# Gated attention block on one core: row sums in the addition, variance by Square, a second buffer of x in the memory of contexts 0 and 1, and the next x's statistics in the middle of a batch

## The reference, cut

```python
# x (4, 512, 512), ctx (4, 512, 256), Wq, Wk (128, 256), weight (512, 512)
def block(x, ctx, g_xattn, g_ffn, ...):
    q = ctx @ Wq.T + bq;  k = ctx @ Wk.T + bk
    attention = softmax(q @ k.T)                       # 512 x 512 per batch
    x = x + tanh(g_xattn) * (layernorm(x) @ attention.T)
    h = layernorm(x)                                    # no affine part
    mean = h.mean(-1);  var = ((h - mean) ** 2).mean(-1)
    hn = (h - mean) * rsqrt(var + 1e-5) * ln_weight + ln_bias
    out = hn @ sign(weight).T * max(abs(weight)) * gamma + beta
    return x + tanh(g_ffn) * out
```

## Time and profile before

| | |
|---|---|
| median of 3 runs | 136.47 us (136.22 to 136.49) |
| the profiled execution: own time, span | 135.49 us, 133.7 us |
| granted TensorE clock in it | 0.999 of full speed |
| busy: PE, DVE | 120.2 us (90%), 114.4 us (86%) |
| busy: POOL, ACT | 85.3 us (64%), 77.5 us (58%) |

### The profile page before, as it was taken

The page is one execution under the profiler, slowest core; times in us unless marked ns, Lnnn a source line. Parts: engine busy times, 40 slices in busy tenths (PEclk is TensorE's granted clock), DMA queues, the critical chain, the costliest instruction groups (busy, mean ns, idle before and its releaser), DMA issues. The chain is left out here.

```text
span 133.7 us, 1815 instructions
## 1 busy us (share of the span) xinstructions
PE 120.2 (90%) x558; PEld 93.6 (70%) x558; DVE 114.4 (86%) x212; ACT 77.5 (58%) x152; POOL 85.3 (64%) x78
## 2 busy tenths in 40 slices
...
GB/s 79 247 178 403 390 385 202 0 54 147 199 24 135 116 40 72 11 83 230 199 179 14 159 78 5 78 235 159 195 40 153 82 5 78 78 78 0 0 157 157
DMA packets 10648, 17.15 MB, mean 128 GB/s; under 512 B 1808, under 2 KB 2576, under 8 KB 10640
## 3 DMA queue, kind: packets, MB, share of 16 engines
...
HBM read 12.59 MB, written 4.19 MB: 126 GB/s over the span
## 5 line engine op out<-in xcount | busy, mean ns | idle before, releaser
L861 POOL TENSOR_TENSOR xt_lo<-xt_raw,xt_hi 128x512 fp32r<-128x512 f32 x16 | 21.5, 1348 | 13.8 <-ACT xt_hi L508 9.3
L872 POOL TENSOR_TENSOR x<-x,shift 128x512 f32<-128x512 f32 x16 | 20.5, 1287 | 7.6 <-DVE zw L684 7.6
L877 POOL TENSOR_TENSOR x<-x,ffn 128x512 f32<-128x512 f32 x14 | 18.4, 1319 | 2.0 <-DVE ffn L716 2.0
L361 PE MATMUL ps_y<-pt_hi,xt_hi 128*128 128x512 f32 x64 | 18.1, 405 | 1.2 <-issue 1.1
L525 ACT ACTIVATE x_sb<-x_sb,y_bias 128x512 f32<-128x512 f32 x16 | 10.3, 718 | 14.9 <-DVE y_bias L664 14.9
L684 DVE SCALAR_TENSOR_TENSOR zw<-x,mv,ln_w 128x512 f32<-128x512 f32 x16 | 18.4, 1150 | 0.4
L374 PE MATMUL ps_ffn<-w_sign,zt_hi 128*128 128x512 f32 x60 | 17.4, 411 | 0.4 <-DVE ffn L716 0.4
L361 PE MATMUL ps_y<-pt_hi,xt_lo 128*128 128x512 f32 x64 | 17.5, 395 | 0.0
L361 PE MATMUL ps_y<-pt_lo,xt_hi 128*128 128x512 f32 x64 | 17.5, 395 | 0.0
L536 ACT ACTIVATE zt_hi<-ps_turn 128x512 fp32r<-128x512 f32 x16 | 9.5, 595 | 13.6 <-PE ps_turn L328 13.4
L374 PE MATMUL ps_ffn<-w_sign,zt_lo 128*128 128x512 f32 x60 | 16.5, 396 | 0.0
...
## 6 DMA issues: line engine op xcount, KB each, us to landing
...
```

Source lines behind the costliest of these rows:

```text
L361: mm = pe.matmul(ps_y[t % 2][:, :], lhs[:, t, k, :], rhs[:, k, :], start=(k == 0 and i == 0), stop=(k == KN - 1 and i == 2))
L861: nc.gpsimd.tensor_tensor(xt_lo[:, t, :, :], xt_raw[:, t, :, :], xt_hi[:, t, :, :].bitcast(f32), ALU.subtract).then_inc(xt_lo_done, 1)
L872: nc.gpsimd.tensor_tensor(x1[:, t, :], x1[:, t, :], shift[:, :], ALU.add).then_inc(x1b_done, 1)
L877: nc.gpsimd.tensor_tensor(x1[:, t, :], x1[:, t, :], ffn[:, t % 2, :], ALU.add)\
```

## The change

- `add_y` also writes the row sum of x1 (`accum_out=sum2`). `mean_x1` becomes one TENSOR_SCALAR on one element per partition, -sum2/N; BN_STATS, the drain and BN_AGGR of x1 go.
- The variance of x1 is taken by ACT: `square_x1`, a Square with bias -mean and its row sum. `var_both` goes from DVE; `power2` on POOL first makes var2 of it. `add_shift` waits for the square as well, since it overwrites x1.
- `var_x` and `scale_x` leave DVE; POOL's new `scale_x` does both and the power, seven instructions a batch (five for batch 0).
- x of odd batches goes into the memory of contexts 0 and 1 (`x_buf`), which is free once batch 1's q is projected: x(1) is loaded in the prologue, x(b+2) when x1(b) is done.
- The statistics of the next x move ahead: DVE's tile 2 before `add_y(b, 2)`, tile 3 right after `mean_x1(b, 3)`; ACT's tile 1 right after `turned_ffn_hi(b, 1)`; the first two tiles of `bias_x` before the last `split_xt`.
- In batch 0 the maximum of the weight is spread before scores(1, 2), and `gain` is scaled on DVE in one instruction instead of two on POOL.

```diff
+        x_buf = (x_sb, ctx_sb[:, 0:2, :, :].rearrange("p b k l -> p (b k) l"))
...
             def load_x(b, t):
-                sp.dma_start(x_sb[:, t, :], x[b, t * P:(t + 1) * P, :]).then_inc(x_in[t], 16)
+                sp.dma_start(x_buf[b % 2][:, t, :], x[b, t * P:(t + 1) * P, :]).then_inc(x_in[b % 2][t], 16)
...
+            sp.wait_ge(proj_ready, 3)
+            sp.wait_ge(ctx_lo_done, 1)
+            for t in range(T):
+                load_x(1, t)
+
             def load_next(b, t):
-                sp.wait_ge(x1_done, T * b + t + 1)
-                load_x(b + 1, t)
+                if b + 2 < B:
+                    sp.wait_ge(x1_done, T * b + t + 1)
+                    load_x(b + 2, t)
                 sp.wait_ge(xt_lo_done, T * b + t + 1)
                 load_xt(b + 1, t)
 
...
+                if is_first(b):
+                    spread_max()
                 scores(b + 1, 2)
                 scores(b + 1, 3)
-                if is_first(b):
-                    spread_max()
...
+            def square_x1(b, t):
+
+                act.wait_ge(mean2_done, T * b + t + 1)
+                if T * b + t > 0:
+                    act.wait_ge(square2_done, T * b + t)
+                nc.scalar.activation(unread[:, 2, :], x1[:, t, :], ACT.Square, bias=neg_mean2[:, t:t + 1],
+                                     accum_out=sq_sum2[:, t:t + 1]).then_inc(square2_done, 1)
+
+            def bias_x(b, tiles):
+                act.wait_ge(ln1_done, 2 * b + 2)
+                for t in tiles:
...
                 normalise(b + 1, 0)
                 turned_ffn_hi(b, 0)
+                square_x1(b, 0)
                 normalise(b + 1, 1)
                 turned_ffn_hi(b, 1)
+                square_x1(b, 1)
+                stats_x(b + 1, 1)
                 exps(b + 1, 2)
...
                 turned_prob_hi(b + 1, 2)
-                stats_x(b + 1, 1)
+                square_x1(b, 2)
                 turned_prob_hi(b + 1, 3)
+                square_x1(b, 3)
                 split_xt(b + 1, 1)
                 split_xt(b + 1, 2)
                 turned_ffn_hi(b, 3)
+                bias_x(b + 1, (0, 1))
                 split_xt(b + 1, 3)
-                bias_x(b + 1)
+                bias_x(b + 1, (2, 3))
...
             def add_y(b, t):
                 dve.wait_ge(out_stored[t], 16 * (b + 1))
                 dve.wait_ge(x_biased, T * b + t + 1)
                 dve.wait_ge(y_ready, T * b + t + 1)
                 nc.vector.scalar_tensor_tensor(out=x1[:, t, :], in0=ps_y[t % 2][:, :],
-                                               scalar=y_scale[:, t:t + 1], in1=x_sb[:, t, :],
-                                               op0=ALU.mult, op1=ALU.add).then_inc(x1_done, 1)
+                                               scalar=y_scale[:, b % 2, t:t + 1], in1=x_buf[b % 2][:, t, :],
+                                               op0=ALU.mult, op1=ALU.add,
+                                               accum_out=sum2[:, t:t + 1]).then_inc(x1_done, 1)
 
             def mean_x1(b, t):
                 dve.wait_ge(x1_done, T * b + t + 1)
-                nc.vector.bn_stats(st2[:, t, :], x1[:, t, :]).then_inc(stat2, 1)
-                dve.drain()
-                nc.vector.bn_aggr(mv2[:, t, :], st2[:, t, :]).then_inc(stat2, 1)
+                nc.vector.tensor_scalar(neg_mean2[:, t:t + 1], sum2[:, t:t + 1], -1.0 / N, None, ALU.mult)\
+                         .then_inc(mean2_done, 1)
 
             def centre(b, t):
-                dve.wait_ge(stat2, STAT2 * b + 2 * t + 2 + t // HALF)
-                nc.vector.scalar_tensor_tensor(out=zw[:, t, :], in0=x1[:, t, :], scalar=mv2[:, t, 0:1],
-                                               in1=ln_w[:, :], op0=ALU.subtract, op1=ALU.mult)\
+                dve.wait_ge(mean2_done, T * b + t + 1)
+                nc.vector.scalar_tensor_tensor(out=zw[:, t, :], in0=x1[:, t, :], scalar=neg_mean2[:, t:t + 1],
+                                               in1=ln_w[:, :], op0=ALU.add, op1=ALU.mult)\
                          .then_inc(zw_done, 1)
-
-            def var_both(b, half):
-
-                cols = slice(half * HALF, (half + 1) * HALF)
-                nc.vector.tensor_scalar(var2[:, cols], mv2[:, cols, 1], 1.0 + EPS, EPS * EPS,
-                                        ALU.mult, ALU.add).then_inc(stat2, 1)
...
                 invert(b + 1, 1)
-                var_both(b, 0)
                 if is_first(b):
                     weight_max(3)
                     dve.wait_ge(wmax_done, KN)
                     nc.vector.tensor_reduce(w_max[:, :], w_maxes[:, :], AX.X, ALU.max).then_inc(wmax_done, 1)
                 turned_ffn_lo(b, 0)
+                stats_x(b + 1, (2,))
                 add_y(b, 2)
                 row_max(b + 1, 2)
                 turned_ffn_lo(b, 1)
-                row_max(b + 1, 3)
                 if is_first(b):
                     dve.wait_ge(max_spread, 1)
                     nc.vector.tensor_reduce(w_scale[:, :], ps_ffn[0][:, :P], AX.X, ALU.max).then_inc(scale_done, 1)
+                    dve.wait_ge(scale_done, 1)
+                    dve.wait_ge(tanh_done, 2)
+                    nc.vector.tensor_scalar(gain[:, :], gain[:, :], w_scale[:, 0:1], tanh_g[:, 1:2],
+                                            ALU.mult, ALU.mult).then_inc(gain_done, 1)
+                row_max(b + 1, 3)
                 mean_x1(b, 2)
                 invert(b + 1, 2)
                 centre(b, 2)
                 invert(b + 1, 3)
-                stats_x(b + 1, (2,))
                 add_y(b, 3)
                 mean_x1(b, 3)
+                stats_x(b + 1, (3,))
                 turned_ffn_lo(b, 2)
                 scale_ffn(b, 0)
                 turned_prob_lo(b + 1, 0)
                 centre(b, 3)
-                var_both(b, 1)
                 turned_prob_lo(b + 1, 1)
                 turned_prob_lo(b + 1, 2)
                 turned_prob_lo(b + 1, 3)
-                stats_x(b + 1, (3,))
-                var_x(b + 1)
                 scale_ffn(b, 1)
                 turned_ffn_lo(b, 3)
-                scale_x(b + 1)
...
                 pool.wait_ge(zw_done, T * b + t + 1)
+                pool.wait_ge(square2_done, T * b + t + 1)
                 nc.gpsimd.tensor_tensor(x1[:, t, :], x1[:, t, :], shift[:, :], ALU.add).then_inc(x1b_done, 1)
...
-            def power1(b):
+            def scale_x(b):
+
+                first = is_first(b)
+                cols = slice(0 if first else HALF, T)
+                if not first:
+                    pool.wait_ge(square1_done, HALF * b)
+                    nc.gpsimd.tensor_scalar(var1[:, :HALF], sq_sum1[:, :HALF], 1.0 / N, EPS,
+                                            ALU.mult, ALU.add).then_inc(var1_done, 1)
+                pool.wait_ge(stat1, 2 * T + 2 * HALF * b)
+                nc.gpsimd.tensor_scalar(var1[:, cols], mv1[:, cols, 1], 1.0, EPS, ALU.mult, ALU.add)\
+                         .then_inc(var1_done, 1)
                 pool.wait_ge(var1_done, 2 * b + 1)
                 nc.gpsimd.tensor_tensor(rstd1[:, :], var1[:, :], neg_half[:, :], ALU.pow)\
-                         .then_inc(rstd1_done, 1)
+                         .then_inc(power1_done, 1)
+                pool.wait_ge(power1_done, b + 1)
+                if b > 1:
+                    pool.wait_ge(x1_done, T * (b - 1))
+                nc.gpsimd.tensor_tensor(y_scale[:, b % 2, :], rstd1[:, :], tanh_g[:, 0:1].broadcast_to([P, T]),
+                                        ALU.mult).then_inc(ln1_done, 1)
+                nc.gpsimd.tensor_tensor(y_back[:, :], rstd1[:, :], tanh_g[:, 2:3].broadcast_to([P, T]),
+                                        ALU.mult).then_inc(scale1_done, 1)
+                pool.wait_ge(scale1_done, max(2 * b, 1))
+                if not first:
+                    pool.wait_ge(ln1_done, 2 * b + 1)
+                    nc.gpsimd.tensor_tensor(y_bias[:, :HALF], neg_mean1[:, :HALF], y_scale[:, b % 2, :HALF], ALU.mult)\
+                             .then_inc(scale1_done, 1)
+                nc.gpsimd.tensor_tensor(y_bias[:, cols], mv1[:, cols, 0], y_back[:, cols], ALU.mult)\
+                         .then_inc(ln1_done, 1)
 
             def power2(b, half):
 
-                pool.wait_ge(stat2, STAT2 * b + (half + 1) * (2 * HALF + 1))
+                pool.wait_ge(square2_done, T * b + (half + 1) * HALF)
                 cols = slice(half * HALF, (half + 1) * HALF)
+                nc.gpsimd.tensor_scalar(var2[:, cols], sq_sum2[:, cols], (1.0 + EPS) / N, EPS * EPS,
+                                        ALU.mult, ALU.add).then_inc(var2_done, 1)
+                pool.wait_ge(var2_done, 2 * b + half + 1)
                 nc.gpsimd.tensor_tensor(rstd2[:, cols], var2[:, cols], neg_half[:, cols], ALU.pow)\
                          .then_inc(rstd2_done, 1)
 
@@ -895,12 +913,12 @@
                 if b > 0:
                     power2(b, 0)
                 split_xt(b + 1, 0)
+                scale_x(b + 1)
```

(15 more changed lines are left out.)

69 lines of the change are left out of this document (23 added, 46 removed).

## The result

The changed kernel takes **132.5 us** (median of 4 runs, 132.16 to 133.26) against 136.47 before: ratio 0.972, 95% interval 0.9675 to 0.9767, so 4.0 us less. The profiled execution took 132.29 us, span 130.8, against 135.49 and 133.7.

The account below looks back on a forecast made before the run. DVE was taken to set the pace for 6.1 us, PE for the rest; 6.1 less 1.1 lost at the end gave 5.0 us, so 130.5 profiled and 131.5 us median, with an 8-in-10 range of 129.6 to 134.8.

Parts of the forecast that it names:

- the difference of 0.98 between profile and median: Before, the profiled execution lay 0.98 us below the median; the same difference was assumed for the changed kernel.
- DVE bounds the turns: At the batch turns PE waits for DVE, which sets the pace for 6.1 us in all.
- So PE's waits of 6.1 us go: With less work on DVE, PE's idle in batches 0 to 2, 6.1 us in all, disappears.
- My walk: Batch 1's turn followed from feed(0, 3): scale_ffn(0, 3) ends near 56.9, centre at 58.5 free or 60.4 blocked.
- It just fits: At batch 1's turn centre ends by 60.4 even if blocked, and PE wants zw at 60.46.
- The end, 1.1: After the last batch power2 waits for ACT's square of tile 3; the last addition starts 1.1 us later, bounds 0.7 to 1.6.
- Durations: Assumed per instruction: mean 0.3 us with its wait, accumulator write 0.1, POOL's small ones 0.3, squares 0.75 with accumulator read.
- POOL goes to 20.8: Eight small instructions at 0.3 us add 2.4 a batch to POOL, from 18.4 to 20.8 of 25.5.
- scale_x off DVE: Moving scale_x from DVE to POOL takes 2.5 us a batch off DVE's work.
- B: Rival: POOL blocks the one-element mean on DVE, then centre again; 133.6 us at half the places, 135.7 at worst; chance 0.18.
- C: Rival: POOL's small instructions cost 1.0 us each, delaying its queue and scale_ffn(b, 2); 139 to 142.1 us, slower; chance 0.09.
- D: Rival: squares on ACT delay exps(b+1, 2), centre(b, 2) and turn_ffn(b, 2) by 1 to 1.5 us a batch; 134.5 to 136; chance 0.08.

Follow-up runs that it names:

- row sums alone: The changed kernel with var_x and scale_x back on VectorE and the next x's statistics at their old places: 131.05 us, ratio 0.959.
- BN_STATS of x1 again: The changed kernel with BN_STATS and BN_AGGR of x1 back in place of the row sum, one-element mean and ScalarE's squares: 134.4 us.

## Why the prediction came out as it did

It said 131.5 us and faster; measured were 132.5. That this is so near is in part luck. Between the two profiled executions the forecast was 5.0 us and 3.2 were measured: the three batches gave 3.4 of the 6.1, and 1.0 came from a prologue that the sum didn't have. The medians differ by 4.0, more than the profiles, since the profiled execution of before had no fall of the clock and most others of that kernel probably had one (last section). Taking over the difference of 0.98 between profile and median was right for before; for the changed kernel it is 0.21. Point by point:

- **DVE bounds the turns: right.** Row sums, squares and gain on DVE alone take 5.6 us off (row sums alone, ratio 0.959).
- **"So PE's waits of 6.1 us go": the step that failed.** The 1.9 us of batch 0 and the 1.67 of batch 2 went. Batch 1's 2.52 became 2.28 with 1.49 of low clock behind it. My walk had scale_ffn(0, 3) ending near 56.9 because of PE's feed, 0.1 us after the start of attend(1, 1) at 56.79. Counted the same way it ended 3.7 us after it (57.19 against 53.47), because of add_ffn(0, 1). I had listed scale_ffn(b, 2)'s waits and not those of tile 3, which writes the other ffn buffer. With four ffn buffers it still ends 1.5 us after it (56.04 against 54.53), since scale_ffn(0, 2) ahead of it waits for power2(0, 1): that wait I had listed and not walked. "It just fits" left 0.06 us if centre was blocked and 2.0 if not, on a queue of GpSimd that I hadn't walked. centre was blocked in part (1.46).
- **The prologue gave 1.0 that I hadn't counted**, 0.7 of it by when the first transfers landed, which is not of the change. It hid as much of the miss: luck.
- **The end, 1.1: measured 1.16.** Row sums and squares are 0.73 of it (BN_STATS of x1 again).
- **Durations.** Mean 0.3, measured 0.145; the accumulator's read 0.1, measured 0.082, and a row of its own, as the page "VectorE: DVE Perf Modes" of the Trainium skill has it in the section "Two Vector instructions with no wait between them"; small ones on POOL 0.3, measured 0.19 to 0.23 (y_bias's first half 0.5); squares 0.72. DVE 20.4 a batch, measured 19.4 to 20.0.
- **POOL.** "POOL goes to 20.8": about right as a sum (22.3 in that batch; 7.0 more over the span, where three batches of 2.4 make 7.2) and wrong as a use of it. What counted was what stands in its queue ahead of add_ffn(b, 1), about 1.5 us. "scale_x off DVE" was booked as a gain of 2.5 a batch; it was a loss of about 2 in all (2.1 by the medians, 1.8 by the ratios).
- **Rivals.** B didn't happen, for a reason I hadn't found. C's price was off (0.2, not the 0.7 at which it decides), but its chain was the one at work: small POOL instructions, then scale_ffn late. D: behind the prologue PE has no wait over 0.6 us but that for zw(1, 0), so exps weren't one.
